# Self-attention of a decoder: who copies the eight weighed blocks out of PSUM

## Chip, cores and metric

One core of a Trainium2 chip runs the whole kernel. The metric is the device time of the kernel in microseconds. The engines are TensorE (PE; PEld is its weight load), VectorE (DVE), ScalarE (ACT), GpSimd (POOL) and SyncE (SP). Each takes its instructions in order from a queue of its own; semaphores hold an instruction back until others have finished.

## What is computed

Two decoder layers on x of shape (8, 256, 256) with a context of (8, 120, 256), all in float32. Layer 0 is self-attention with 16 heads of width 64, cross-attention with 16 heads of width 16, and a quantized gated MLP; layer 1 has another attention, a cross-attention and a coupled feed-forward net. Each part is followed by a sum and a layer norm. The change concerns layer 0's self-attention alone:

```python
q = jnp.einsum('bsm,hmd->bhsd', x, kernel[0])
k = jnp.einsum('bsm,hmd->bhsd', x, kernel[1])
v = jnp.einsum('bsm,hmd->bhsd', x, kernel[2])
scores = jnp.einsum('bhsd,bhtd->bhst', q, k) * scale
attn = jax.nn.softmax(scores, axis=-1)
out = jnp.einsum('bhst,bhtd->bhsd', attn, v)
out = jnp.transpose(out, (0, 2, 3, 1)).reshape(b, s, d * h)
out = jnp.einsum('bsf,fm->bsm', out, WO[0])
```

## The kernel before

The batch of 8 is done in four passes of two sequences (it = 0 to 3). A pass runs self-attention, cross-attention and MLP of layer 0, then the parts of layer 1, written out by hand for each engine; each engine has a function attn0 that lists its share of the self-attention in order. Work of the neighbouring passes is woven in: the projections for the next pass, and the last norm and output of the pass before.

The self-attention goes over 16 units (U0 = 16). Unit u is head pair j = u // 2 of sequence b = u % 2. attn0 counts rounds u = 0 to 17, and in round u the engines do the following.

- PE (L1095 on): scores of unit u+1 (scores0, L656, into PSUM banks 0 to 3), the weighing of the values of unit u-2 (weigh0, L692, into one half of bank 6), and the transposes of unit u-1 (turn0, L676, into banks 4 and 5). The scores of a unit wait until the exponentials two units before have left the bank; the transposes wait for POOL. Rounds 6 and 8 also carry the two context projections (L728, L735); in pass 0 rounds 9 to 16 carry matmuls that fold norm gains into weights (fold_bias, fold_mean). Rounds 15 to 17 begin the output projection (out0, L710), and after the last round comes the rest of it.
- ACT (L1364): the exponentials of unit u with their sums (exp0, L1342), in rounds 3, 5, ..., 17 the copy of a weighed block (keep_o0, L1356), and half of the copy of the transposed unit u-1 (keep_e0t, L1352).
- DVE (L1749): the maxima of unit u+1 (max0, L1717), the inverses of the sums of unit u (inverse0, L1723), the other half of the copy of the transposed unit u-1 (keep_e0t, L1738), and then extra work: in passes 1 to 3 coefficients, scaling, sums and norms of the pass before in rounds 0, 4, 5, 7, 9 and 11, a context copy each in rounds 6 and 8, and in pass 0 the folds in rounds 11, 14 and 17.
- POOL (L2254): a short pause instruction (L2229), then four multiplies by the inverses of unit u (L2262), in place. It waits for the inverses.

A weighed block is bank 6 whole: head pair j of both sequences, 128 partitions by 512. It is complete when the weighing of unit 2j+1 is done, in round 2j+3, and is copied to o0t (the room of the queries, in SBUF). There are eight of them (j = 0 to 7) in a pass. PE waits for the copy before the weighing of unit 2j+2, which writes bank 6 anew, in the next round, and before the output projection, which reads o0t. The weighing itself waits for both halves of the copy of the transposed unit. The inverses share DVE's queue with everything else on DVE: they can't start before what stands ahead of them there.

Of the kernel before, what the change touches and what calls it, by code (L numbers as in the profile page):

```python
# [39 lines left out]
def first_pass(it):  # L40

    return isinstance(it, int) and it == 0


def decoder(nc, I, out):
# [6 lines left out]
    NB = 2  # L52
# [17 lines left out]
    with ExitStack() as es:  # L70
# [3 lines left out]
        def signal(name, per=1):  # L74
            return Signal(es.enter_context(nc.semaphore(name)), per)
# [13 lines left out]
        def bank(n):  # L89
            return PS[:, n, :]  # L90
# [115 lines left out]
        o0t = q0  # L206
# [142 lines left out]
        av0_done, o0_kept = signal("av0_done", U0), signal("o0_kept", J)  # L349
# [76 lines left out]
        def half_of(tile, g):  # L426

            return tile.rearrange("p h t (s e i) -> p (h t s) e i", e=2, i=64)[:, :, g, :]
# [869 lines left out]
        def _(act):  # L1298
# [28 lines left out]
            def keep_k0(it, j):  # L1327
                act.wait_ge(k0_done.sem, k0_done.at(it, j + 1))
                act.copy(k0[:, j, :, :].rearrange("p b s -> p (b s)"), bank(KEY_FILL[j])).then_inc(k0_kept.sem, 1)
# [12 lines left out]
            def exp0(it, u):  # L1342
                for hh in range(2):
                    act.wait_ge(m0_done.sem, m0_done.at(it, 2 * u + hh + 1))
                    if u > 1:
                        act.wait_ge(t0_done.sem, t0_done.at(it, u - 1))
                    for st in range(TS):
                        op = act.activation(e0[:, u % 2, st, hh, :], bank(2 * (u % 2) + hh)[:, st * S:(st + 1) * S], ACT.Exp,  # L1348
                                            bias=nmax0[:, u % 2, hh, st:st + 1], accum_out=sum0[:, u % 2, hh, st:st + 1])
                    op.then_inc(p0_done.sem, 1)  # L1350

            def keep_e0t(it, u):  # L1352
                act.wait_ge(t0_done.sem, t0_done.at(it, u + 1))
                act.copy(half_of(e0t[:, u % 2, :, :, :], 1), bank(5).rearrange("p (a i) -> p a i", i=64)).then_inc(t0_kept_a.sem, 1)  # L1354

            def keep_o0(it, j):  # L1356
                act.wait_ge(av0_done.sem, av0_done.at(it, NB * (j + 1)))
                act.copy(o0t[:, j, :], bank(6)).then_inc(o0_kept.sem, 1)  # L1358

            def load_table(function):  # L1360

                act.activation(table_probe[:, 0:1], minus_magic[:, 0:1], function, scale=0.0)

            def attn0(it, last=None):  # L1364
                if last is None:
                    load_table(ACT.Exp)
                for u in range(U0 + 2):
                    if u < U0:
                        exp0(it, u)
                    if last is not None and u in (0, 1):  # L1370
                        keep_k0(it, J - 2 + u)
                    if u >= 2 and u % 2 == 1:
                        keep_o0(it, (u - 2) // 2)
                    if 1 <= u <= U0:
                        keep_e0t(it, u - 1)

# [267 lines left out]
        def _(dve):  # L1644
# [29 lines left out]
            def of(tile):  # L1674
                return lambda t: tile[:, t, :]
# [41 lines left out]
            def max0(it, u):  # L1717
                for hh in range(2):
                    dve.wait_ge(s0_done.sem, s0_done.at(it, 2 * u + hh + 1))
                    dve.tensor_reduce(nmax0[:, u % 2, hh, :], bank(2 * (u % 2) + hh).rearrange("p (t s) -> p t s", t=TS), AX.X, ALU.max,  # L1720
                                      negate=True).then_inc(m0_done.sem, 1)

            def inverse0(it, u):  # L1723
                dve.wait_ge(p0_done.sem, p0_done.at(it, 2 * (u + 1)))
                if u > 1:
                    dve.wait_ge(n0_done.sem, n0_done.at(it, u - 1))
                dve.reciprocal(inv0[:, u % 2, :, :], sum0[:, u % 2, :, :]).then_inc(i0_done.sem, 1)  # L1727
# [10 lines left out]
            def keep_e0t(it, u):  # L1738
                dve.wait_ge(t0_done.sem, t0_done.at(it, u + 1))
                dve.tensor_copy(half_of(e0t[:, u % 2, :, :, :], 0), bank(4).rearrange("p (a i) -> p a i", i=64)).then_inc(t0_kept_v.sem, 1)  # L1740

            def keep_context_values(it, kv):
                dve.wait_ge(v1_done.sem, v1_done.at(it, kv + 1))
                for b in range(NB):
                    op = dve.tensor_tensor(v1[:, kv, b, :], bank(MLP_OUT[kv])[0:M, b * D:(b + 1) * D],
                                           row["L1_xattn_bv%d" % (kv + 1)][0:M, :], ALU.add)
                op.then_inc(v1_kept.sem, 1)

            def attn0(it, last=None, then=None):  # L1749
                for u in range(U0 + 2):  # L1750
                    if u + 1 < U0:
                        max0(it, u + 1)
                    if u < U0:
                        inverse0(it, u)
                    if 1 <= u <= U0:
                        keep_e0t(it, u - 1)
                    if last is not None and u == 0:
                        keep_coef(last, 1)
                    if last is not None and u == 4:
                        scale_out(last, 1)  # L1760
                    if last is not None and u == 5:
                        add_out(last, 1)
                    if last is not None and u == 7:
                        apply_norm(last, "out", of(res), y, 0)
                    if last is not None and u == 9:
                        norm_summed(last, "out", 1)
                    if last is not None and u == 11:
                        apply_norm(last, "out", of(res), y, 1)
                    if u == 6:
                        dve.wait_ge(kx_done.sem, kx_done.at(it, 1))  # L1770
                        for c in range(KD):
                            op = dve.tensor_scalar(kx[:, c, :], bank(7)[:, c * NC:(c + 1) * NC], col["L0_xattn_bk"][:, c:c + 1],
                                                   None, ALU.add)
                        op.then_inc(kx_kept.sem, 1)
                    if u == 8:
                        dve.wait_ge(vx_done.sem, vx_done.at(it, 1))
                        for b in range(NB):
                            op = dve.tensor_tensor(vxp[:, b, :, ::2, :],
                                                   bank(7)[0:M, b * D:(b + 1) * D].rearrange("p (a e d) -> p a e d", e=2, d=DH),
                                                   row["L0_xattn_bv"][0:M, :].rearrange("p (a e d) -> p a e d", e=2, d=DH), ALU.add)  # L1780
                        op.then_inc(vx_kept.sem, 1)
                    if first_pass(it) and u in (11, 14, 17):
                        fold_norm((u - 11) // 3)
# [371 lines left out]
            def keep_coef(it, b):  # L2155
                h = slice(TS * b, TS * b + TS)
                dve.wait_ge(final_turned.sem, final_turned.at(it, b + 1))
                dve.tensor_copy(coef[:, h, :], bank((7, 6)[b])[:, 0:TS * P].rearrange("p (t q i) -> p t q i", t=TS, i=32)[:, :, 0:3, 0]
                                ).then_inc(coef_kept.sem, 1)
# [5 lines left out]
            def scale_out(it, b):  # L2165
                h = slice(TS * b, TS * b + TS)
                dve.wait_ge(coef_kept.sem, coef_kept.at(it, b + 1))
                dve.tensor_tensor(cross_coef[:, h, :], coef[:, h, 0:2], coef[:, h, 2:3].to_broadcast([P, TS, 2]), ALU.mult
                                  ).then_inc(coef_crossed.sem, 1)
                dve.wait_ge(coef_crossed.sem, coef_crossed.at(it, b + 1))  # L2170
                dve.scalar_tensor_tensor(out=out_coef[:, h, 0], in0=coef[:, h, 0], scalar=1.0, in1=cross_coef[:, h, 1],
                                         op0=ALU.add, op1=ALU.subtract)
                dve.tensor_tensor(out_coef[:, h, 1], coef[:, h, 1], cross_coef[:, h, 0], ALU.add).then_inc(coef_ready.sem, 1)
                dve.wait_ge(coef_ready.sem, coef_ready.at(it, b + 1))
                for t in range(TS * b, TS * b + TS):
                    op = dve.tensor_scalar(res[:, t, :], xs["5"][:, t, :], out_coef[:, t, 0:1], None, ALU.mult)
                op.then_inc(x5_scaled.sem, 1)
# [257 lines left out]
```

## Time and profile before

| | |
|---|---|
| median of 3 runs | 1188.82 us (1186.34 to 1189.29) |
| the profiled execution | 1191.58 us, span 1189.4 us |
| PE busy | 1060.7 us (89%) |
| PE weight loads | 691.1 us (58%) |
| DVE busy | 772.1 us (65%) |
| ACT busy | 652.4 us (55%) |
| POOL busy | 322.7 us (27%) |

The profile is of one execution, and its times of single instructions are taken from that. Busy times overlap, since the engines work side by side; what a change is worth depends on which engine ends the wait at its place. A matmul's end is modelled, and the granted clock of PE is given as a share of 2.4 GHz. In the timeline, one row can stand for several instructions of one line that follow each other (x8); the number in brackets is the idle time of the engine before the row, with what ended it.

### The profile page before, as it was taken

What the parts mean: (1) busy time and instruction counts of PE and PEld (TensorE: products, weight loads), DVE (VectorE), ACT (ScalarE), POOL (GpSimd) and SP (SyncE); (2) the same over time, 40 slices, a digit from 0 to 9 for tenths busy, and PEclk for the clock granted to TensorE, in tenths of its full rate; (3) what the DMA queues carried; (4) which work ended last, traced back from release to release, by engine and by line L of the source; (5) the groups of instructions that cost most, each with busy time, mean ns of one, the idle gap of its engine ahead of it and who ended that gap; (6) DMA issues with size and microseconds to landing.
All of it is one profiled execution on the core that took longest, in us unless ns stands there. A gap on an engine that the chain in (4) does not pass through costs nothing.

```text
span 1189.4 us, 19960 instructions
## 1 busy us (share of the span) xinstructions
PE 1060.7 (89%) x7313; PEld 691.1 (58%) x7313; DVE 772.1 (65%) x1866; ACT 652.4 (55%) x1744; POOL 322.7 (27%) x670
## 2 busy tenths in 40 slices
PE   7899888999899988899899999899989997789985
PEld 3466544775656744675566654477565564477552
DVE  0764478557778468565857657755867837955776
ACT  2475256348478455546658734635847835434843
POOL 1154301131136410232025630113014641023111
PEclk9999899999999999998999999999999999999998
DMA  9630000000000000000000000000000000000000
GB/s 274 175 94 1 18 1 9 1 1 1 1 18 2 19 19 1 9 1 1 2 1 19 19 18 2 9 1 1 2 1 1 20 1 2 1 1 1 2 1 18
DMA packets 30496, 22.79 MB, mean 19 GB/s; under 512 B 16704, under 2 KB 29504, under 8 KB 30272
## 3 DMA queue, kind: packets, MB, share of 16 engines
q1 hardware_dynamic: 29952, 21.50, 6.6%
q8 instruction: 59, 0.97, 0.3%
q14 instruction: 37, 0.30, 0.1%
q10 hardware_dynamic: 448, 0.02, 0.0%
HBM read 19.42 MB, written 2.10 MB: 18 GB/s over the span
## 4 chain that ended last, share of the span: by engine, by line
PE 59%; DVE 20%; ACT 10%; issue 6%; POOL 4%; DMA 0%; SPq 0%; POOLq 0%; DVEq 0%; ACTq 0%
PE PS L554 7%; PE PS L719 5%; PE PS L541 4%; PE PS L964 4%; PE PS L705 3%; PE PS L591 3%; ACT work L1533 3%; PE PS L807 3%; PE PS L688 3%; PE PS L670 2%; POOL work L2262 2%; PE PS L938 2%; PE PS L977 2%; ACT work L1348 2%; DVE work L1844 2%
## 5 line engine op out<-in xcount | busy, mean ns | idle before, releaser
L2234 POOL TENSOR_TENSOR rstd<-var,minus_half 128x2 f32<-128x2 f32 x64 | 46.2, 722 | 436.6 <-DVE var L1661 436.2
L1533 ACT ACTIVATE work<-PS,nmax 120x256 f32<-120x256 f32 x256 | 118.1, 485 | 25.6 <-DVE nmax L2072 24.6
L2262 POOL TENSOR_SCALAR work<-work,inv 128x256 f32<-128x256 f32 x256 | 119.7, 487 | 0.0
L1348 ACT ACTIVATE work<-PS,nmax 128x256 f32<-128x256 f32 x256 | 118.3, 483 | 1.1 <-DVE nmax L1720 1.1
L2072 DVE TENSOR_REDUCE nmax<-PS 120x2 f32<-120x512 f32 x128 | 82.7, 685 | 44.2 <-PE PS L964 43.9
L1720 DVE TENSOR_REDUCE nmax<-PS 128x2 f32<-128x512 f32 x128 | 82.2, 684 | 20.0 <-PE PS L670 19.8
L2229 POOL TENSOR_TENSOR pool_pause<-minus_half 128x1 f32<-128x1 f32 x96 | 30.3, 315 | 227.5 <-DVE inv L1727 116.0
L964 PE MATMUL PS<-x_room 32*120 32x256 f32 x512 | 68.7, 401 | 12.7 <-ACT work L1533 8.8
L670 PE MATMUL PS<-work 64*128 64x256 f32 x512 | 74.2, 401 | 1.9 <-ACT work L1348 1.9
L705 PE MATMUL PS<-work 128*64 128x256 f32 x512 | 70.3, 396 | 1.5 <-DVE work L1740 1.1
L964 PEld LDWEIGHTS PS<-x_room 32*120 32x120 f32 x512 | 42.1, 178 | 40.5 <-issue 33.0
L1740 DVE COPY work<-PS 128x512 f32<-128x512 f32 x64 | 43.8, 685 | 28.6 <-PE PS L688 28.3
L719 PE MATMUL PS<-wo,work 128*128 128x256 f32 x256 | 59.6, 385 | 2.7 <-ACT work L1358 2.7
L1830 DVE TENSOR_REDUCE maxx<-PS 128x8 f32<-128x960 f32 x32 | 36.9, 1153 | 36.9 <-PE PS L778 36.9
L1304 ACT COPY turned_a<-PS 128x512 f32<-128x512 f32 x24 | 14.2, 592 | 82.0 <-PE PS L524 81.9
L688 PEld LDWEIGHTS PS<-ident,work 64*128 64x128 f32 x1024 | 37.6, 141 | 33.8 <-POOL work L2262 22.8
L1667 DVE TENSOR_SCALAR x_room<-res,mv,rstd 128x256 f32<-128x256 f32 x96 | 36.3, 420 | 30.8 <-POOL rstd L2234 30.8
L1533 ACT ACTIVATION_READ_ACCUMULATOR work<-PS,nmax 120x1 f32 x256 | 55.4, 216 | 0.0
L1348 ACT ACTIVATION_READ_ACCUMULATOR work<-PS,nmax 128x1 f32 x256 | 54.9, 214 | 0.0
L1354 ACT COPY work<-PS 128x512 f32<-128x512 f32 x64 | 37.6, 587 | 29.9 <-PE PS L688 28.7
L719 PEld LDWEIGHTS PS<-wo,work 128*128 128x128 f32 x256 | 47.4, 190 | 11.1 <-ACT work L1358 4.6
L670 PEld LDWEIGHTS PS<-work 64*128 64x128 f32 x512 | 46.9, 190 | 11.6 <-ACT work L1348 5.6
(280 smaller groups left out, 2441.2 us busy)
## 6 DMA issues: line engine op xcount, KB each, us to landing
turned_x<-in_xT_dram SPq DMA_DIRECT2D x8, 256.0 KB, 3.0
xa<-in_x_dram SPq DMA_DIRECT2D x4, 512.0 KB, 3.9
rows<-in_rows_dram SPq DMA_DIRECT2D x1, 1536.0 KB, 13.5
late<-in_L_attn_W_dram SPq DMA_DIRECT2D x2, 768.0 KB, 7.9
out_dram<-x_room SPq DMA_DIRECT2D x3, 512.0 KB, 3.4
wv<-in_L_attn_kernel_dram SPq DMA_DIRECT2D x4, 256.0 KB, 5.1
wq<-in_L_attn_kernel_dram SPq DMA_DIRECT2D x2, 512.0 KB, 7.2
wk<-in_L_attn_kernel_dram SPq DMA_DIRECT2D x2, 512.0 KB, 7.6
```

The lines of the kernel that those rows point to most:

```text
L541: mm = pe.matmul(bank(n)[:, c * S:(c + 1) * S], weight[:, k, c * P:(c + 1) * P], src[:, k, b * S:(b + 1) * S], start=(k == 0), stop=(k == ...
L554: mm = pe.matmul(bank(n)[:, (t % 2) * width:(t % 2 + 1) * width], lhs[:, k, t * P:(t + 1) * P], weight[:, k, :], start=(k == 0), stop=(k = ...
L670: mm = pe.matmul(bank(2 * (u % 2) + hh)[:, st * S:(st + 1) * S], q0[rows, j, b * S + st * P:b * S + (st + 1) * P], k0[rows, j, b, :], star ...
L688: mm = pe.transpose(bank(4 + g)[:, place:place + 64], e0[rows, u % 2, st, hh, tt * P:(tt + 1) * P], ident[rows, rows])
L705: mm = pe.matmul(bank(6)[hh * DH0:(hh + 1) * DH0, b * S:(b + 1) * S], v0[:, TS * b + tt, (2 * j + hh) * DH0:(2 * j + hh + 1) * DH0], e0t[: ...
L719: mm = pe.matmul(bank(t // 2)[:, (t % 2) * D:(t % 2 + 1) * D], o0t[:, j, t * P:(t + 1) * P], wo0[:, j, :], start=(j == 0), stop=(j == J - 1))
L964: mm = pe.matmul(bank(SCORE_1[r])[0:M, kv * S:(kv + 1) * S], k1m[g % 2][rows, kv, par, :], q1[rows, c, b * S:(b + 1) * S], start=True, sto ...
L1348: op = act.activation(e0[:, u % 2, st, hh, :], bank(2 * (u % 2) + hh)[:, st * S:(st + 1) * S], ACT.Exp, bias=nmax0[:, u % 2, hh, st:st + 1 ...
L1533: op = act.activation(e1[:, par, r, kv, :], bank(SCORE_1[r])[0:M, kv * S:(kv + 1) * S], ACT.Exp, bias=nmax1[:, par, r, kv:kv + 1], accum_o ...
L1720: dve.tensor_reduce(nmax0[:, u % 2, hh, :], bank(2 * (u % 2) + hh).rearrange("p (t s) -> p t s", t=TS), AX.X, ALU.max, negate=True).then_i ...
L2072: dve.tensor_reduce(nmax1[:, par, r, :], bank(SCORE_1[r])[0:M, :].rearrange("p (v s) -> p v s", v=2), AX.X, ALU.max, negate=True).then_inc ...
L2262: op = pool.tensor_scalar(e0[:, u % 2, st, hh, :], e0[:, u % 2, st, hh, :], inv0[:, u % 2, hh, st:st + 1], 1.0, ALU.mult, ALU.mult)
```

## The change

The helper keep_o0 moves from ACT's program to DVE's, as a tensor_copy in place of an activation copy, with the same wait, the same source, the same destination and the same signal. ACT's attn0 no longer calls it. DVE's attn0 calls it in the same rounds, 3, 5, ..., 17, behind the maxima of the next unit and ahead of the inverses of the round's own. Nothing else is changed.

```diff
--- before.py
+++ after.py
@@ -1353,10 +1353,6 @@
                 act.wait_ge(t0_done.sem, t0_done.at(it, u + 1))
                 act.copy(half_of(e0t[:, u % 2, :, :, :], 1), bank(5).rearrange("p (a i) -> p a i", i=64)).then_inc(t0_kept_a.sem, 1)
 
-            def keep_o0(it, j):
-                act.wait_ge(av0_done.sem, av0_done.at(it, NB * (j + 1)))
-                act.copy(o0t[:, j, :], bank(6)).then_inc(o0_kept.sem, 1)
-
             def load_table(function):
 
                 act.activation(table_probe[:, 0:1], minus_magic[:, 0:1], function, scale=0.0)
@@ -1369,8 +1365,6 @@
                         exp0(it, u)
                     if last is not None and u in (0, 1):
                         keep_k0(it, J - 2 + u)
-                    if u >= 2 and u % 2 == 1:
-                        keep_o0(it, (u - 2) // 2)
                     if 1 <= u <= U0:
                         keep_e0t(it, u - 1)
 
@@ -1739,6 +1733,10 @@
                 dve.wait_ge(t0_done.sem, t0_done.at(it, u + 1))
                 dve.tensor_copy(half_of(e0t[:, u % 2, :, :, :], 0), bank(4).rearrange("p (a i) -> p a i", i=64)).then_inc(t0_kept_v.sem, 1)
 
+            def keep_o0(it, j):
+                dve.wait_ge(av0_done.sem, av0_done.at(it, NB * (j + 1)))
+                dve.tensor_copy(o0t[:, j, :], bank(6)).then_inc(o0_kept.sem, 1)
+
             def keep_context_values(it, kv):
                 dve.wait_ge(v1_done.sem, v1_done.at(it, kv + 1))
                 for b in range(NB):
@@ -1750,6 +1748,8 @@
                 for u in range(U0 + 2):
                     if u + 1 < U0:
                         max0(it, u + 1)
+                    if u >= 2 and u % 2 == 1:
+                        keep_o0(it, (u - 2) // 2)
                     if u < U0:
                         inverse0(it, u)
                     if 1 <= u <= U0:
```

## Rows read from the trace of the kernel before

**Rows 1.** Page, part 4: the chain that ended last, its share of the span by engine.
```profile
PE 59%; DVE 20%; ACT 10%; issue 6%; POOL 4%; DMA 0%; SPq 0%; POOLq 0%; DVEq 0%; ACTq 0%
```

**Rows 2.** Windows view, pass 1's self-attention: stretch, length, busy (instructions) PE, PEld, DVE, ACT, POOL, clock, DMA.
```profile
352.00:404.00 52.00, 49.13 (x524) 32.13 (x518) 35.44 (x77) 39.49 (x137) 31.01 (x76) 1.00 0.07 22
```

**Rows 3.** Waits view, the same stretch: waiter <- releaser: us in total, times, longest.
```profile
PE PS L688 <- POOL work L2262: 1.9, 5, 0.8
```

**Rows 4.** Timeline, pass 1, rounds 3 and 4: start, us, engine, line, instruction, idle before.
```profile
355.91 1.08 PE L705 MATMUL PS<-work 128*64 128x256 f32 x8
...
356.01 1.29 DVE L1720 TENSOR_REDUCE nmax<-PS 128x2 f32<-128x512 f32 x2 [0.34 <-PE PS L670]
...
357.15 0.71 PE L688 MATMUL PS<-ident,work 64*128 64x64 f32 x16 [0.16 <-POOL work L2262]
...
357.27 0.61 ACT L1358 COPY work<-PS 128x512 f32<-128x512 f32 x1
...
357.43 0.18 DVE L1727 RECIPROCAL inv<-sum 128x4 f32<-128x4 f32 x1
...
357.90 0.59 ACT L1354 COPY work<-PS 128x512 f32<-128x512 f32 x1
...
358.39 0.48 ACT L1348 ACTIVATE work<-PS,nmax 128x256 f32<-128x256 f32 x1
...
358.82 1.29 DVE L1720 TENSOR_REDUCE nmax<-PS 128x2 f32<-128x512 f32 x2 [0.22 <-PE PS L670]
...
359.76 0.71 PE L688 MATMUL PS<-ident,work 64*128 64x64 f32 x16
...
360.36 0.18 DVE L1727 RECIPROCAL inv<-sum 128x4 f32<-128x4 f32 x1 [0.26 <-ACT work L1348]
...
360.52 0.69 DVE L1740 COPY work<-PS 128x512 f32<-128x512 f32 x1
```

**Rows 5.** Timeline, pass 1, round 5.
```profile
361.13 0.15 DVE L2168 TENSOR_TENSOR cross_coef<-coef 128x4 f32<-128x4 f32 x1
...
362.73 1.27 DVE L1720 TENSOR_REDUCE nmax<-PS 128x2 f32<-128x512 f32 x2
...
363.92 0.16 DVE L1727 RECIPROCAL inv<-sum 128x4 f32<-128x4 f32 x1
...
366.56 0.72 PE L688 MATMUL PS<-ident,work 64*128 64x64 f32 x16 [0.76 <-POOL work L2262]
```

**Rows 6.** Timeline, pass 1, rounds 11 and 13.
```profile
382.80 1.29 DVE L1720 TENSOR_REDUCE nmax<-PS 128x2 f32<-128x512 f32 x2
...
384.22 0.18 DVE L1727 RECIPROCAL inv<-sum 128x4 f32<-128x4 f32 x1
...
387.00 0.71 PE L688 MATMUL PS<-ident,work 64*128 64x64 f32 x16
...
388.82 1.29 DVE L1720 TENSOR_REDUCE nmax<-PS 128x2 f32<-128x512 f32 x2 [0.29 <-PE PS L670]
...
390.21 0.18 DVE L1727 RECIPROCAL inv<-sum 128x4 f32<-128x4 f32 x1
...
392.69 0.71 PE L688 MATMUL PS<-ident,work 64*128 64x64 f32 x16
```

**Rows 7.** Timeline, pass 1, round 15 and the stage's end.
```profile
395.90 0.18 DVE L1727 RECIPROCAL inv<-sum 128x4 f32<-128x4 f32 x1 [1.76 <-ACT work L1348]
...
399.00 0.71 PE L688 MATMUL PS<-ident,work 64*128 64x64 f32 x16
...
403.56 0.59 ACT L1358 COPY work<-PS 128x512 f32<-128x512 f32 x1 [3.22 <-PE PS L705]
...
404.20 8.90 PE L719 MATMUL PS<-wo,work 128*128 128x256 f32 x40 [0.69 <-ACT work L1358]
```

**Rows 8.** Timeline, pass 0, round 9.
```profile
85.65 0.17 DVE L1727 RECIPROCAL inv<-sum 128x4 f32<-128x4 f32 x1
...
89.15 0.71 PE L688 MATMUL PS<-ident,work 64*128 64x64 f32 x16
```

## The prediction

> **What bounds the kernel now.** I read the page's chain first, then one self-attention stage by its window, its waits and its rows in order of time. The chain that ended last lies on PE for 59% and on DVE for 20%, on ACT for 10% and on POOL for 4% [rows 1]. So a copy taken off ACT is worth something only where ACT ends a wait inside this one stage. The stage of pass 1 lasts 52 us; PE is busy for 49.13 of them, ACT for 39.49, DVE for 35.44, at a granted clock of 1.00, which is the 2.4 GHz level [rows 2]. Of PE's idle time there, 1.9 us in five waits are waits for POOL's multiplies before the transposes [rows 3].
>
> The rows of rounds 3 and 4 show why PE waits [rows 4]. A loop closes every two rounds. I measure its links from start to start. Inverses of round 3 at 357.43, its transposes at 359.76: 2.33 (POOL's pause and four multiplies lie between). From transposes to ACT's copy of the turned block, 357.15 to 357.90: 0.75. Copy to exponentials, 357.90 to 358.39: 0.49. Exponentials to their inverses, 358.39 to 360.36: 1.97. Sum 5.54 for two rounds. ACT's copy of the weighed block (357.27, 0.61 us) is in none of these links: it runs while ACT would anyway wait for transposes that start at 357.15 and end at 357.86, and the copy of the turned block starts at 357.90, some 0.04 after.
>
> **The change, part by part.** *Removed:* 32 ACT copies (eight in each of four passes) of 0.59 to 0.61 us. Worth at most 0.04 us where they touch the loop [rows 4], and the seven that have rounds around them are followed by the copy of a turned block that PE releases. I take 0. The other end would be that all of PE's 1.9 us of waits in a pass go [rows 3], 7.6 us over four passes.
>
> *Added:* 32 DVE copies of the same 128x512 shape. DVE's copy of a turned block out of the same memory takes 0.69 us, and lets the next instruction start after 0.61 (360.52 to 361.13) [rows 4, 5]. What matters is the place: between the maxima of the next round and this round's inverses. DVE's queue runs in order, so behind the new copy stand the inverses (for which POOL waits, and then PE's transposes), DVE's copy of the turned block, and the extra work of that round. The copy's own wait, for the weighing of two rounds back, costs nothing: the weighing begins at 355.91 and lasts 1.08, the maxima begin at 356.01 and last 1.29 [rows 4].
>
> Now the odd rounds have a second loop. The transposes of unit u are followed on PE by the scores of unit u+3, whose maxima stand on DVE right ahead of the new copy and the inverses of unit u+2. Transposes to those maxima, 357.15 to 358.82: 1.67 [rows 4]. Two maxima let the next instruction start after 1.19 to 1.21 (362.73 to 363.92) [rows 5]; I take 1.20. The new copy: 0.61. Inverses to transposes: 2.33. Sum 5.81, against 5.54. Before, this loop was 5.20, hidden under the other. So an undisturbed pair of rounds grows by 0.27 us, and more where other work had already brought DVE behind.
>
> I lay pass 1 out round by round. The new inverses come 1.20 + 0.61 = 1.81 after the start of the maxima.
> - Round 3: maxima at 356.01, inverses at 357.82 and not 357.43: 0.39 late, and so are the transposes 2.33 later [rows 4].
> - Round 5: the DVE copy of round 3's block waits for these transposes, and behind it coefficients and a scaling of the last pass run without a gap into the maxima at 362.73, which slip by 0.39. Inverses at 362.73 + 0.39 + 1.81 = 364.93 for 363.92: 1.01 late. The transposes at 366.56 were released by POOL and slip as much [rows 5].
> - Rounds 7 and 9: the two context projections stand on PE behind transposes of odd rounds, and the maxima behind them, so all slips with PE; in each the maxima-to-inverses time of 1.20 becomes 1.81. Lateness 1.6, then 2.2.
> - Round 11: transposes of round 9 now at 383.2, maxima at 384.89 (before 382.80), inverses at 386.70 for 384.22, transposes at 389.03 for 387.00: only 2.0, since these had stood behind PE's own work with some 0.4 to spare [rows 6].
> - Round 13: maxima 1.78 to 1.82 behind the transposes, at 390.81 for 388.82; inverses at 392.62 for 390.21; transposes at 394.95 for 392.69: 2.26 late [rows 6].
> - Round 15: no maxima precede the copy; the inverses at 395.90 move by about 0.7, but their transposes start 3.10 later, at 399.00, against 2.33 needed: covered [rows 7].
> - Last copy: at 403.56, with PE waiting 0.69 for it until 404.20 [rows 7]. It takes 0.69 instead of 0.59: 0.10 on the path.
>
> Pass 1: 2.26 + 0.10 = 2.36 us. Passes 2 and 3 repeat pass 1's order of work: I take the same. In pass 0 the fold matmuls stand ahead of some transposes: the inverses of round 9 start at 85.65, their transposes at 89.15, 3.50 later, so 1.17 of cover [rows 8]. There round 9 costs nothing, and round 13, which has the same matmuls ahead, neither. Round 3 costs the 0.40 of pass 1; round 5 the loop's 0.27, as DVE has no work of a last pass; rounds 7 and 11, whose maxima wait for PE, 0.61 each; the exit 0.10: 1.99 us. Sum: 3 x 2.36 + 1.99 = 9.1 us. PE works without slack from here to the stage's end and the later stages start from its outputs, so I let all of it reach the end.
>
> The profiled execution took 1191.58 us (span 1189.40, with 2.18 around it); the sum makes it 1200.7. The median of the runs before is 1188.82, 2.8 below that execution; on the median the forecast is 1197.9.
>
> **A rule of the skill against the rows.** In this stage ACT is busy for 39.49 us and DVE for 35.44 [rows 2]. The Trainium skill (TensorEngine Tiling (Array Packing), PSUM Bottleneck) says to use both ScalarE and VectorE to empty PSUM. Read as a call for balance, it speaks for this move. By it the stage would lose some of PE's 1.9 us of waits per pass, down to 1181 at its furthest. The rows speak against it here, as both engines are idle for over 12 us and the order on DVE, not its load, decides. It is the first rival.
>
> **Rivals.**
> 1. *ACT was the late one.* If freeing ACT by 0.6 us in every second round lets exponentials start earlier, PE's waits for POOL shrink. Bounds: 0 to 1.9 us in each pass, 1181.2 at the far end. It decides only if ACT's copy of a turned block now starts before its old time after the transposes. For: ACT has the second highest load. Against: in round 3 that distance is 0.75 from the start of the transposes, and 0.04 from their end [rows 4].
> 2. *The copy is hidden (no change).* The late inverses are absorbed wherever POOL is ahead of PE, as in round 15 of pass 1 and round 9 of pass 0 [rows 7, 8], and only the exits cost, 4 x 0.10: 1189.2. It decides if PE has over 0.4 us of queued work ahead of the transposes in most rounds. Against: the rows of rounds 3 and 5, where PE idles for POOL (0.76 in round 5) [rows 5].
> 3. *Dearer.* The whole 0.69 stays on the path in each of six rounds and none is absorbed: 6 x 0.69 + 0.10 = 4.24 in a pass, 17.0 in all, 1205.8. For: with the copy DVE has hardly a gap in rounds 5 to 13, so every slip may add up. Against: rounds 11 and 13, where the rows show cover. PE's longer waits could also bring the clock down to 1.2 GHz for a while; before, the stage held 1.00 with waits of up to 0.76 [rows 2, 5], so I give this no time of its own.
>
> **How the numbers follow.** Forecast 0.68, rival 1 0.04, rival 2 0.12, rival 3 0.16. A difference below 0.3%, 3.6 us, can't be told from no change. The forecast's own range: with the copy at 0.69 instead of 0.61 and the maxima 1.78 instead of 1.67 behind the transposes, six rounds give up to 0.5 to 0.8 us more in a pass, 1201; with two more rounds covered in each pass, some 4 us less, 1194. So 1194 to 1201, all of it slower by over 0.3%. To hold 8 in 10 the range must take in rival 3 and come near rival 2: 1191 to 1206. Slower: 0.68 + 0.16, less 0.02 for a sum that fails low: 0.82. Same: 0.12 and a little of the forecast and of rival 1: 0.13. Faster: 0.05.
>
> **What would show it.** In the changed trace the inverses of odd rounds should start about 1.8 us behind their maxima, right at the end of the new copy, those of even rounds still wait for ACT or follow the maxima by 1.2. The new copy itself should show next to no wait for the weighing, except in rounds 15 and 17. PE's waits for POOL's multiplies should grow from 1.9 to about 4 us in a pass, in the odd rounds, with the distance from inverses to transposes still at 2.33. ACT should idle longer before its copies of turned blocks, with its busy time down by some 19 us. It is wrong if the odd inverses are late but the scores aren't (cover), if POOL's multiplies grow in length, or if the time goes up in another stage.

## Result and profile after

The changed kernel takes 1196.90 us (median of 5 runs, 1193.45 to 1198.80), the kernel before 1188.82 us (1186.34 to 1189.32). The ratio is 1.0064, with a 95% interval of 1.0050 to 1.0079: slower, by 8.1 us between the medians. The forecast was 1197.9. Single executions far above the rest (1202.97 and 3598.47 us in experiment 7, 2099.77 in its runs of the kernel before) are left out of all ratios.

The profiled execution took 1196.90 us, its span is 1194.7 us: 5.3 us over the span before. In the chain that ended last DVE now has 22% for 20 and POOL 5% for 4, ACT 9% for 10 and PE 58% for 59 (part 4 of the page of the changed kernel, answers to [rows 1]).

```profile
PE 58%; DVE 22%; ACT 9%; POOL 5%; issue 5%; DMA 0%; SPq 0%; POOLq 0%; DVEq 0%; ACTq 0%
```

The windows view of pass 1's self-attention in the changed kernel (columns as in [rows 2]) shows ACT's load down, DVE's up (the two have about changed places), and PE with as much work in 54 us as it had in 52:

```profile
351.00:405.00 54.00, 49.01 (x522) 31.93 (x516) 39.74 (x85) 35.32 (x129) 30.97 (x76) 1.00 0.06 21
```

Its waits view for the same stretch (waiter <- releaser: us in total, times, longest), to set beside [rows 3]:

```profile
ACT work L1354 <- PE PS L688: 14.9, 15, 2.6
...
PE PS L688 <- POOL work L2262: 3.2, 8, 0.8
...
PE PS L705 <- DVE work L1734: 1.1, 1, 1.1
```

PE waits 3.2 us in eight waits for POOL's multiplies, where it was 1.9 in five. The prediction had named about 4 for these waits, so that sign came out short. PE also waits 1.1 us before a weighing, where it was 0.4 and where nothing had been forecast; together the two kinds grew by 2.0 us, about the 2.1 that the stage grew by. ACT waits 14.9 us before its copies of turned blocks (5.8 before): the time that it was relieved of has become idle time.

The timeline of the changed kernel, pass 1, round 3 (start, us, engine, line, instruction, idle before), answers to [rows 4]. L1714 are the maxima, L1738 the moved copy, L1721 the inverses, L688 the transposes of unit 3, L1734 DVE's copy of the turned block:

```profile
354.94 1.29 DVE L1714 TENSOR_REDUCE nmax<-PS 128x2 f32<-128x512 f32 x2 [0.34 <-PE PS L670]
...
356.15 0.68 DVE L1738 COPY work<-PS 128x512 f32<-128x512 f32 x1
...
356.75 0.17 DVE L1721 RECIPROCAL inv<-sum 128x4 f32<-128x4 f32 x1
...
359.07 0.71 PE L688 MATMUL PS<-ident,work 64*128 64x64 f32 x16 [0.34 <-POOL work L2262]
...
359.82 0.69 DVE L1734 COPY work<-PS 128x512 f32<-128x512 f32 x1 [0.35 <-PE PS L688]
```

The inverses stand 1.81 us behind the start of the maxima (1.42 before), and the transposes 2.32 behind the inverses. Nothing but the copy has come between. Round 5, answers to [rows 5]:

```profile
361.23 0.75 DVE L2176 TENSOR_SCALAR res<-x_room,out_coef 128x256 f32<-128x256 f32 x2
...
361.89 1.28 DVE L1714 TENSOR_REDUCE nmax<-PS 128x2 f32<-128x512 f32 x2
...
363.09 0.68 DVE L1738 COPY work<-PS 128x512 f32<-128x512 f32 x1
...
363.69 0.17 DVE L1721 RECIPROCAL inv<-sum 128x4 f32<-128x4 f32 x1
...
364.48 1.08 PE L705 MATMUL PS<-work 128*64 128x256 f32 x8 [1.06 <-DVE work L1734]
...
366.33 0.71 PE L688 MATMUL PS<-ident,work 64*128 64x64 f32 x16 [0.76 <-POOL work L2262]
```

Again 1.80 from maxima to inverses (1.19 before). The weighing at 364.48 has waited 1.06 us for the copy of the turned block. Four rows of the kernel before, to set beside these: POOL's multiplies of unit 4, the scaling (L2176), the same weighing after 0.37 us, and the context projection behind it, of which experiment 8 tells.

```profile
360.79 1.88 POOL L2262 TENSOR_SCALAR work<-work,inv 128x256 f32<-128x256 f32 x4
...
361.83 0.98 DVE L2176 TENSOR_SCALAR res<-x_room,out_coef 128x256 f32<-128x256 f32 x2
...
364.72 1.08 PE L705 MATMUL PS<-work 128*64 128x256 f32 x8 [0.37 <-DVE work L1740]
...
367.21 1.89 PE L728 MATMUL PS<-ctxt,x0TWk 128*128 128x240 f32 x8
```

Rounds 11 and 13, answers to [rows 6], and round 15 and the exit, answers to [rows 7]:

```profile
383.67 1.29 DVE L1714 TENSOR_REDUCE nmax<-PS 128x2 f32<-128x512 f32 x2 [0.22 <-PE PS L670]
...
385.47 0.17 DVE L1721 RECIPROCAL inv<-sum 128x4 f32<-128x4 f32 x1
...
387.86 0.71 PE L688 MATMUL PS<-ident,work 64*128 64x64 f32 x16 [0.21 <-POOL work L2262]
...
389.52 1.29 DVE L1714 TENSOR_REDUCE nmax<-PS 128x2 f32<-128x512 f32 x2 [0.21 <-PE PS L670]
...
391.33 0.17 DVE L1721 RECIPROCAL inv<-sum 128x4 f32<-128x4 f32 x1
...
393.65 0.71 PE L688 MATMUL PS<-ident,work 64*128 64x64 f32 x16
```

```profile
397.52 0.17 DVE L1721 RECIPROCAL inv<-sum 128x4 f32<-128x4 f32 x1
...
399.94 0.71 PE L688 MATMUL PS<-ident,work 64*128 64x64 f32 x16
...
404.51 0.69 DVE L1738 COPY work<-PS 128x512 f32<-128x512 f32 x1 [3.12 <-PE PS L705]
...
405.26 6.96 PE L719 MATMUL PS<-wo,work 128*128 128x256 f32 x31 [0.79 <-DVE work L1738]
```

Since pass 1 starts at another time in the two traces, I count from the maxima of unit 4 (356.01 before, 354.94 after). How much later than before the transposes of the units start, beside the lateness that I had laid out:

| unit | predicted, us | measured, us |
|---|---|---|
| 3 | 0.39 | 0.38 |
| 5 | 1.01 | 0.84 |
| 7 | 1.6 | 1.46 |
| 9 | 2.2 | 2.06 |
| 11 | 2.0 | 1.93 |
| 13 | 2.26 | 2.03 |
| rest of the output projection | 2.36 | 2.13 |

Rounds 3 to 9 carry all of it: four steps of 0.38, 0.46, 0.62 and 0.60 make 2.06, rounds 11 to 15 add nothing on balance, and the exit adds 0.10.

Taken the same way, pass 0 grew by 1.94 us (1.99 predicted; its steps were 0.39, 0.25, 0.60 and 0.60 in rounds 3, 5, 7 and 11 and nothing in rounds 9 and 13), pass 3 by 2.13, pass 2 by 3.73. Pass 2 has something else in it: a stretch in which PE's clock was at 1.2 GHz, and of which experiment 8 tells. Without that the four passes sum to 3 x 2.13 + 1.94 = 8.3 us. The spans differ by less, 5.3 us, because such stretches also lie differently in the two executions elsewhere. Ahead of the maxima of unit 4 in pass 0 the changed one had gained 2.2 us (the granted clock from 52 to 66 us of the span is 0.88, where it was 0.76), and all that lies between the self-attentions took 2.4 us less, with two stretches at 1.2 GHz (near 128 and 548 us) half as long as before.

### The profile page after: what moved, and what is told of

The parts are those of the page before. It is cut to its first block, busy times and chain, and to the rows that moved or that the text cites. A ratio compares the mean times of both kernels' runs of the same rounds, so it can differ in the third digit from the quotient of the medians.

```text
span 1194.7 us, 19926 instructions
## 1 busy us (share of the span) xinstructions
PE 1053.9 (88%) x7279; PEld 689.4 (58%) x7313; DVE 789.6 (66%) x1898; ACT 635.2 (53%) x1712; POOL 322.7 (27%) x670
## 4 chain that ended last, share of the span: by engine, by line
PE 58%; DVE 22%; ACT 9%; POOL 5%; issue 5%; DMA 0%; SPq 0%; POOLq 0%; DVEq 0%; ACTq 0%
PE PS L554 7%; PE PS L719 5%; PE PS L541 4%; PE PS L964 4%; POOL work L2262 4%; PE PS L670 3%; PE PS L591 3%; ACT work L1527 3%; PE PS L807 3%; PE PS L688 2%; PE PS L938 2%; PE PS L977 2%; DVE nmax L1714 2%; DVE work L1844 2%; PE PS L705 2%
## 5 line engine op out<-in xcount | busy, mean ns | idle before, releaser
L1714 DVE TENSOR_REDUCE nmax<-PS 128x2 f32<-128x512 f32 x128 | 82.2, 684 | 19.9 <-PE PS L670 19.7
L705 PE MATMUL PS<-work 128*64 128x256 f32 x512 | 69.4, 392 | 3.6 <-DVE work L1734 3.2
L688 PEld LDWEIGHTS PS<-ident,work 64*128 64x128 f32 x1024 | 37.3, 140 | 39.1 <-POOL work L2262 31.6
L1734 DVE COPY work<-PS 128x512 f32<-128x512 f32 x64 | 43.5, 680 | 21.2 <-PE PS L688 20.2
L688 PE MATMUL PS<-ident,work 64*128 64x64 f32 x1024 | 46.2, 231 | 12.1 <-POOL work L2262 11.7
```

Source lines behind the costliest of these rows:

```text
L688: mm = pe.transpose(bank(4 + g)[:, place:place + 64], e0[rows, u % 2, st, hh, tt * P:(tt + 1) * P], ident[rows, rows])
L705: mm = pe.matmul(bank(6)[hh * DH0:(hh + 1) * DH0, b * S:(b + 1) * S], v0[:, TS * b + tt, (2 * j + hh) * DH0:(2 * j + hh + 1) * DH0], e0t[: ...
```

## Experiments

For the comparison of all kernels I use a stretch whose ends exist in each: in pass 1, from the transposes of unit 0 to the first transposes of the cross-attention. It takes 61.32 us before and 63.44 with the change (+2.12; the expectations count it from the maxima of unit 4 to the rest of the output projection, 48.19 and 50.32, +2.13). Theory 1: the copy costs by its place, ahead of the inverses. Rivals: DVE's added load costs wherever it stands; ACT's relief is worth something. The ratios are to runs of the kernel before on the same chip. Experiments 1 to 4 ran on one chip, 5 to 8 on another.

| | pass 1's stretch, us | against before | ratio of times (95%) |
|---|---|---|---|
| before | 61.32 | | |
| the change | 63.44 | +2.12 | 1.0064 (1.0050 to 1.0079) |
| 1 behind the inverses | 61.75 | +0.43 | 1.0028 (1.0011 to 1.0045) |
| 2 behind the copy of the turned block | 63.97 | +2.65 | 1.0077 (1.0053 to 1.0101) |
| 3 added on DVE, ACT as before | 63.22 | +1.90 | 1.0051 (1.0032 to 1.0070) |
| 4 ACT copies one column | 60.83 | -0.49 | 0.9994 (0.9976 to 1.0011) |
| 5 two copies on DVE | 67.81 | +6.49 | 1.0230 (1.0186 to 1.0274) |
| 6 ahead of the maxima | 68.44 | +7.12 | 1.0236 (1.0201 to 1.0272) |
| 7 before, exit covered | 60.49 | -0.83 | 0.9959 (0.9942 to 0.9977) |
| 8 the change again | 64.99 | +3.67 | 1.0052 (1.0036 to 1.0069) |

The pass is the better measure, since the time of the whole kernel also moves with the mean granted clock of the execution. The kernel before, on the chip of experiments 1 to 4, took 1190.5 to 1191.5 us where that mean was 0.984, 1188.0 to 1188.9 at 0.987 and 1185.6 to 1186.0 at 0.990. At 0.987 the changed kernel took 1196.9 to 1198.8 in the runs of the result: 8 to 11 us more, where the medians say 8.1. (Which chip the result's runs had is not on record.) In the pass two traces of the same work differ by up to 0.1 us: experiment 7 leaves rounds 0 to 16 as they were, and its rounds come out 0.07 shorter than in the trace of the kernel before.

**1. Behind the inverses.**

```diff
+                    if u < U0:
+                        inverse0(it, u)
                     if u >= 2 and u % 2 == 1:
                         keep_o0(it, (u - 2) // 2)
-                    if u < U0:
-                        inverse0(it, u)
```

> The changed kernel with the DVE copy moved one place: behind the inverses of its round, still ahead of DVE's copy of the turned block. I measure the stage of pass 1 from the start of the maxima of unit 4 to the start of the rest of the output projection: 48.19 us in the kernel before, 50.32 in the changed one. Theory 1 (the place: the copy stands ahead of the inverses that POOL and then PE wait for): the odd inverses follow their maxima by 1.2 again and not 1.8. What is late instead is DVE's copy of the turned block, by 0.2 to 0.6 us in the odd rounds, for which the next weighing waits; part of that is hidden. Growth of the stage 1.0 to 1.4 us instead of 2.13, time about 1193.5. Theory 2 (the load: DVE has 0.6 us more to do, wherever it stands): growth 2.1 as before, time about 1197.

Measured: +0.43 us in the pass, of which 0.10 at the exit; 1190.92 us. The load theory falls: the same copy on the same engine costs a fifth. Its timeline, round 3 (L1738 is the copy, L1734 the copy of the turned block, L705 the weighing that needs the latter):

```profile
356.98 0.18 DVE L1721 RECIPROCAL inv<-sum 128x4 f32<-128x4 f32 x1
...
357.08 0.66 DVE L1738 COPY work<-PS 128x512 f32<-128x512 f32 x1
...
357.65 0.68 DVE L1734 COPY work<-PS 128x512 f32<-128x512 f32 x1
...
358.39 1.08 PE L705 MATMUL PS<-work 128*64 128x256 f32 x8
```

The turned block is copied 0.2 us later than ACT's half, and the weighing at 358.39 still needs not wait. In round 6 it does wait, 0.97 us where it was 0.37, but PE's wait for POOL right behind it is 0.27 instead of 0.76, so nearly all of that is hidden. I had expected a growth of 1.0 to 1.4 and so had overrated what the later copy of the turned block does.

**2. Behind the copy of the turned block.**

```diff
-                    if u >= 2 and u % 2 == 1:
-                        keep_o0(it, (u - 2) // 2)
                     if u < U0:
                         inverse0(it, u)
                     if 1 <= u <= U0:
                         keep_e0t(it, u - 1)
+                    if u >= 2 and u % 2 == 1:
+                        keep_o0(it, (u - 2) // 2)
```

> The changed kernel with the DVE copy behind DVE's copy of the turned block, ahead of the round's extra work. Theory 1 (the place): neither the odd inverses nor that copy is late; only rounds 9 and 11, where extra work follows without a gap into the maxima of the next round, pass on up to 0.6 us each. Growth of pass 1's stage 0.7 to 1.5 us, of which 0.1 to 0.2 at the exit; time about 1193. Theory 2 (the load): growth 2.1, time about 1197.

A miss: +2.65, more than the change itself. The inverses are on time, but the timeline of round 3 shows what I had left out:

```profile
356.16 0.69 DVE L1734 COPY work<-PS 128x512 f32<-128x512 f32 x1 [0.30 <-PE PS L688]
...
356.77 0.68 DVE L1738 COPY work<-PS 128x512 f32<-128x512 f32 x1
...
357.60 1.08 PE L705 MATMUL PS<-work 128*64 128x256 f32 x8 [0.56 <-DVE work L1738]
```

The next weighing writes bank 6 anew and waits for the copy out of it: at 357.60, after 0.56 us. Its waits view for the stage has the sum:

```profile
PE PS L705 <- DVE work L1738: 3.7, 6, 0.9
```

So the copy has two deadlines. It stands best behind the inverses and ahead of the copy of the turned block, and even there it is not free. "Out of the way, at the end of the round" was wrong. This result taken alone fits the load theory; with experiment 1 it does not.

**3. Added on DVE, ACT as before.**

```diff
                         max0(it, u + 1)
+                    if u >= 2 and u % 2 == 1:
+                        dve.tensor_reduce(spare[:, :], causal[:, :, :], AX.X, ALU.max)
```

> The kernel before, with ACT's copies kept, and a DVE maximum over 128x512 constants (its result unused) in the changed kernel's place, between the maxima and the inverses of rounds 3, 5, ..., 17. Theory 1: this alone costs what the change costs, but for the exit (0.1 us a pass): odd inverses about 1.8 behind their maxima, growth of pass 1's stage about 2.0, time about 1196. Rival (the removal from ACT gives something back that the change hides): growth clearly above 2.1.

(spare is a tile that only this instruction writes.) +1.90 in the pass, 1194.24 us. The timeline of round 3 (L1755 is the added instruction):

```profile
354.24 1.29 DVE L1721 TENSOR_REDUCE nmax<-PS 128x2 f32<-128x512 f32 x2 [0.33 <-PE PS L671]
...
355.44 0.68 DVE L1755 TENSOR_REDUCE spare<-causal 128x2 f32<-128x512 f32 x1
...
356.04 0.17 DVE L1728 RECIPROCAL inv<-sum 128x4 f32<-128x4 f32 x1
```

The inverses stand 1.80 behind the maxima, as with the change. With the dearer exit (0.10) that makes 2.00 of the change's 2.12. Had ACT's relief given something back, the change would have cost less than this sum, not 0.12 more (and 0.07 of this is how far the repeat of the change in experiment 8 lies below its first trace, 63.38 and 63.36 in passes 2 and 3 for 63.44). The added instruction reads constants in SBUF and not PSUM, so where the copy reads from isn't the cause either.

**4. ACT copies one column.**

```diff
-                act.copy(o0t[:, j, :], bank(6)).then_inc(o0_kept.sem, 1)
+                act.copy(o0t[:, j, 0:1], bank(6)[:, 0:1]).then_inc(o0_kept.sem, 1)
```

> The kernel before with ACT's copy of the weighed block cut to one column of 512; nothing is added on DVE, and the other columns of the weighed blocks are left out, so that this times only what ACT's relief is worth. Theory 1: nothing inside the rounds; only the exit is shorter, by about 0.35 us a pass: stage of pass 1 at 47.8 us, time about 1187.4. Rival (ACT was the late one): exponentials start earlier, PE's waits for POOL of 1.9 us a pass go, stage at 46 to 47 us, time 1181 to 1185.

-0.49 in the pass, 0.42 of it at the exit and 0.07 in all the rounds before, as much as in experiment 7, where ACT's copies are whole: inside the rounds nothing is left for ACT's relief. PE's waits for POOL in its stage stay where they were (1.9 before):

```profile
PE PS L688 <- POOL work L2262: 1.8, 5, 0.7
```

The rival in which ACT was the late one is dead: its far end was 1.9 us a pass.

**5. Two copies.**

```diff
+                dve.tensor_copy(spare[:, :], bank(6))
                 dve.tensor_copy(o0t[:, j, :], bank(6)).then_inc(o0_kept.sem, 1)
```

> The changed kernel with a second DVE copy of bank 6, into an unused tile, right ahead of the real one. Theory (the time stands in DVE's order ahead of the inverses, and little of it is covered): odd inverses 2.4 us behind their maxima; each of rounds 3 to 13 costs another 0.6, round 15 has used up its cover of 0.7 us and costs about 0.5, the exit 0.6: stage of pass 1 at about 55.0 us (50.32 with one copy, 48.19 before), time about 1215. Rival (a fixed price of the wait between engines, whatever the copy's length): stage at 50.3 to 51.5, time 1197 to 1202.

+6.49, where 6.8 was expected; 1213.77 us. Round 3:

```profile
357.37 1.29 DVE L1715 TENSOR_REDUCE nmax<-PS 128x2 f32<-128x512 f32 x2 [0.34 <-PE PS L671]
...
358.57 0.68 DVE L1739 COPY spare<-PS 128x512 f32<-128x512 f32 x1
...
359.17 0.68 DVE L1740 COPY work<-PS 128x512 f32<-128x512 f32 x1
...
359.77 0.17 DVE L1722 RECIPROCAL inv<-sum 128x4 f32<-128x4 f32 x1
```

2.40 from maxima to inverses. The first copy cost 2.12, the second 4.37: the first one had found slack (0.22 us in round 3, 0.66 in round 15), the second finds little. It adds 0.58 to 0.61 us in rounds 3, 7, 9, 11 and 13 and at the exit, but 0.33 in round 5 and 0.49 in round 15. A price per wait and not per length is ruled out.

**6. Ahead of the maxima.**

```diff
-                    if u + 1 < U0:
-                        max0(it, u + 1)
                     if u >= 2 and u % 2 == 1:
                         keep_o0(it, (u - 2) // 2)
+                    if u + 1 < U0:
+                        max0(it, u + 1)
```

> The changed kernel with the DVE copy ahead of the maxima of its round. There it has to wait for the weighing, which PE does behind the scores that the maxima need, so the maxima themselves are late. Theory (order and waits on DVE's queue set the price): loop of the odd rounds: transposes to scores 0.55, scores and weighing 2.1, copy 0.6, maxima 1.2, inverses to transposes 2.33, some 6.9 us with the delays between engines, against 5.54: 1.3 more in each of six odd rounds, stage of pass 1 at about 56 us, time about 1219. Rival (load alone): stage as in the changed kernel, 50.3.

+7.12 for the 7.8 expected; 1217.20 us. The maxima of unit 4 are themselves late here, so from there on the stage shows only 53.67; from unit 0 on it shows the whole. Round 3:

```profile
363.10 0.69 DVE L1738 COPY work<-PS 128x512 f32<-128x512 f32 x1 [1.37 <-PE PS L705]
...
363.71 1.28 DVE L1714 TENSOR_REDUCE nmax<-PS 128x2 f32<-128x512 f32 x2
...
364.90 0.17 DVE L1721 RECIPROCAL inv<-sum 128x4 f32<-128x4 f32 x1
```

DVE sits idle 1.37 us for a weighing that, in the changed kernel, it finds finished.

**7. Exit covered.** A version of the kernel before that the exit of [rows 7] points to.

```diff
                     if u == U0 + 1:
-                        out0(it, 2, 0, J - 2)
+                        out0(it, 2, 0, 3)
                     if u >= 2:
                         weigh0(it, u - 2, last)
+                    if u == U0 + 1:
+                        out0(it, 2, 3, J - 2)
```

> The kernel before, copies on ACT; only PE's order in round 17 differs: of the twelve output projections that stood ahead of the last weighing, six now stand behind it, where PE had waited 0.69 us for the copy of the last block. Theory: they take 1.5 us, the wait goes: stage of pass 1 at 47.5 us instead of 48.19, four passes 2.8 us, time about 1185.5. Rival: the last weighing, now 1.4 us earlier, has to wait for the copies of the turned block (these end at 400.4, and the weighing would start at about 401.1, so little room), and the gain is nothing: stage at 48.2.

-0.83 in the pass, where 0.7 was expected; 1184.99 us, ratio 0.9959 (0.9942 to 0.9977). This beats both kernels. Four passes make 3.3 us; the ratio says 4.9, and the rest lies with the clock, as 8 of the 19 runs beside it had a mean of 0.984 and none of its own did. At 0.986 it took 1186.7 to 1187.1, the kernel before 1189.4 to 1190.8. In its timeline the output projection runs on behind the last weighing without a wait; it had been 0.69 us:

```profile
397.07 1.56 PE L719 MATMUL PS<-wo,work 128*128 128x256 f32 x6
...
398.56 1.08 PE L705 MATMUL PS<-work 128*64 128x256 f32 x8
...
399.58 10.20 PE L719 MATMUL PS<-wo,work 128*128 128x256 f32 x46
```

**8. The change again.** No edit.

> The changed kernel once more, for a second trace. Theory: pass 1's stage at 50.32 us again, the round-by-round times the same to a few hundredths. What differs between executions is where PE's clock is at its lower level: in the first trace one such stretch lay in the self-attention of pass 2, which took 51.93. If that is chance, it is absent or elsewhere now; if PE's longer waits for POOL cause it, it lies in a self-attention stage again, near rounds 5 to 7.

Maxima to inverses and the starts of the transposes up to unit 5 are the same to 0.04 us. But pass 1 took 64.99 now, and passes 2 and 3 63.38 and 63.36. Timeline around the context projection of round 6 (L728), and windows (columns as in [rows 2]) over it:

```profile
364.37 1.08 PE L705 MATMUL PS<-work 128*64 128x256 f32 x8 [1.04 <-DVE work L1734]
...
366.20 0.84 PE L688 MATMUL PS<-ident,work 64*128 64x64 f32 x16 [0.75 <-POOL work L2262]
...
366.97 3.38 PE L728 MATMUL PS<-ctxt,x0TWk 128*128 128x240 f32 x8
```

```profile
364.00:368.00 4.00, 2.88 (x27) 2.04 (x28) 3.32 (x7) 1.63 (x7) 3.43 (x9) 0.83 0.00 0
368.00:372.00 4.00, 4.00 (x21) 2.79 (x21) 1.39 (x3) 1.50 (x8) 0.72 (x2) 0.75 0.00 0
```

The projection takes 3.38 us where the kernel before needed 1.89, and in the windows the granted clock is 0.83 and 0.75: PE is at 1.2 GHz for a while, right behind two waits of 1.04 and 0.75 us. That is 1.6 us, once. In the first trace of the change it happened at this place in pass 2, in experiment 3 in pass 3; over the three traces with these waits (the change twice and experiment 3) it happened in three of nine passes. It never happened there in passes 1 to 3 of the kernel before or of experiments 1, 4 and 7, twelve passes. But neither did it in experiments 2, 5 and 6, in 5 behind even longer waits of 1.39 and 0.75. That PE's longer idle time favours it is likely; that it causes it is not shown.

## Why the prediction was right

- *What bounds the stage.* The 5.54 us loop without ACT's copy in it was right: shortening that copy to one column changed the rounds by no more than two traces differ (0.07 us, experiments 4 and 7), and I had taken 0. With ACT and DVE both idle for over 12 us of the stage, moving work from the busier to the less busy one cost 2.1; it did not even out their loads but about exchanged them (39.49 and 35.44 us before, 35.32 and 39.74 after). The Trainium skill's advice in TensorEngine Tiling (Array Packing), PSUM Bottleneck, is to use both engines for emptying PSUM. Both kernels do so; read as a call for balance it gives the wrong sign here.
- *The added copy by its place.* 1.81 us from maxima to inverses in all six odd rounds was predicted, 1.80 or 1.81 found. Experiments 1, 3, 5 and 6 show that it is the order on DVE that is paid for.
- *Rounds 3 and 5.* Round 3 is exact. In round 5 I had passed all of the 0.39 on to the maxima; only 0.23 arrived, as the scaling ahead of them (L2176) took 0.66 us from its start to the maxima instead of 0.90. The traces show when it is slow. In the kernel before POOL's multiplies run until 362.67, beside both of its instructions (0.49 and 0.56 us); in the changed one they end at 361.57, beside the first alone (0.49 and 0.34); in experiment 5 they end ahead of it (0.35 and 0.35, 0.53 to the maxima). Passes 1 to 3 of all ten traces agree. This is most of the gap between 2.36 and 2.13.
- *Round 13.* I had set the maxima 1.78 to 1.82 behind the transposes, and they came after 1.66, the shorter of my two rows.
- *An even round between.* The transposes of unit 4 were on time (0.01 us early), though those of unit 3 were 0.38 late. What reached round 5 came, as forecast, through DVE: its copy of unit 3's block, the scaling, the maxima.
- *Cover in round 15 and in pass 0.* Both as predicted: the inverses of unit 15 were 2.69 late where PE was 2.03 late, and their transposes still stood 2.42 behind them, 0.1 more than needed; pass 0 grew by 1.94.
- *The exit.* 0.10, as predicted: PE's wait there went from 0.69 to 0.79.
- *What I missed.* Of PE's longer waits only 3.2 us were for POOL, not about 4, since I had not seen the wait of 1.06 us before the weighing in round 6, grown from 0.37. It needed no term of its own in the sum, since POOL's multiplies ended last there, and PE waited again for these. ACT's busy time fell by 17.2 us and not by some 19. And the clock: I gave it no time, and it took 1.6 us in one pass of each of the three traces with the copy's time ahead of the inverses (the change twice, and experiment 3). That the medians differ by 8.1 us, so near to the 8.3 of the passes, is partly luck, since the granted clock elsewhere moves single executions by some 5 us.
- *The rivals.* Hidden copy (1189.2): excluded, the odd inverses were late and so were the transposes. Dearer (1205.8): the cover of rounds 11, 13 and 15 is real.

## What to carry to other kernels

Before moving work between engines, lay out what stands behind it in the new queue and which loop runs through that: the same eight copies of 0.6 us cost between 0.4 and 7.1 us a pass, depending only on their place in DVE's order. Where they stayed on ACT, they cost nothing inside the rounds. Such a copy has two deadlines, the work queued behind it and the writer that waits for its buffer; both are to be read from the timeline, and the end of the round is not safe. At the end of this stage, where PE had other products at hand, filling its wait gave 0.8 us a pass (experiment 7), and cutting the awaited copy to one column 0.5 (experiment 4).

## What was unexpected of the hardware

- The same program, with the same waits of 1.04 to 1.06 and 0.75 to 0.76 us before the context projection, had PE's clock at 2.4 GHz there in some passes and at 1.2 GHz for some 3 us in others; the granted clock of a 4 us window fell to 0.65 in pass 2 of the first trace.
- The four multiplies of POOL took 1.85 us beside DVE's copies out of PSUM and 2.17 us in round 5, beside DVE's scaling and adding of three operands (L2183), which took 1.12 us there and 0.88 in round 0, with no multiplies beside it. The two instructions of the scaling L2176 took 0.35 us each alone and up to 0.49 and 0.56 beside the multiplies. In all ten traces the scaling, the adding and the multiplies beside the adding were longer where the engines lay beside each other, and POOL's 0.3 us more stood on the path.
